# A selective-scan mixer on one core: dt, B and C from h by folded weights, a shorter softplus series, two units moved between engines, a new order

## The reference, cut to what matters

```
h  = layernorm(x) * (1 + ca) + sa                     # 16 x 512 x 256
xz = h @ W_in.T ;  x_ssm, z = split(xz)               # 512 channels each
B, C = x_ssm @ W_B.T, x_ssm @ W_C.T                   # 16 states each
dt = softplus(x_ssm @ W_dt.T + b_dt)                  # 512 channels
# for every time t, channel d, state n:
s[d,n] = exp(dt[d] * A[d,n]) * s[d,n] + dt[d] * B[n] * x_ssm[d]
y[d]   = sum_n s[d,n] * C[n]
y = (y + x_ssm * D) * silu(z)
x = x + ga * (y @ W_out.T) * sigmoid(output_gate)
```

## Time and profile before

| | us |
|---|---|
| median of three runs | 4714.47 (4711.55 to 4716.5) |
| the profiled execution | 4710.14 |
| its span | 4708.4 |
| granted TensorE clock, mean over the span | 0.972 |
| setup, until the first load of x is issued | 35.45 |
| first scan starts | 114.78 |
| last scan starts | 1960.91 |

### The profile page before, as it was taken

One profiled execution on the slowest core, in us unless ns is written; L12 is line 12 of the kernel. 1 busy time (PEld: TensorE's weight loads), 2 busy tenths in 40 slices (PEclk: granted clock), 3 DMA queues, 4 the chain that ended last, 5 costly groups with the idle time before them and its releaser, 6 DMA issues. The chain is left out here.

```text
span 4708.4 us, 60762 instructions
## 1 busy us (share of the span) xinstructions
PE 4365.9 (93%) x19870; PEld 2651.1 (56%) x19870; DVE 3755.0 (80%) x6094; ACT 2731.8 (58%) x5844; POOL 2231.3 (47%) x1060
## 2 busy tenths in 40 slices
PE   5999999999999999649999999999999999999997
PEld 3444444444444444226676767676666667676665
DVE  2999999999999999667777777777777777777773
ACT  3666666666666666215555656564656556565653
POOL 1999999999999999612111111111111111111110
PEclk7999999999999999869999999999999999999999
DMA  1233333333333333330000000001010000001000
GB/s 65 104 113 113 113 112 113 113 117 116 113 116 114 113 112 108 108 112 9 24 14 28 14 28 15 28 14 54 14 67 19 28 28 24 31 19 37 19 32 23
DMA packets 112567, 299.37 MB, mean 64 GB/s; under 512 B 18940, under 2 KB 39008, under 8 KB 111488
## 3 DMA queue, kind: packets, MB, share of 16 engines
q1 hardware_dynamic: 104240, 283.46, 17.7%
q10 hardware_dynamic: 8016, 12.03, 0.7%
HBM read 254.81 MB, written 40.63 MB: 63 GB/s over the span
## 5 line engine op out<-in xcount | busy, mean ns | idle before, releaser
L840 POOL TENSOR_TENSOR a_state<-a_state,a_c_wide 128x1024 f32<-128x1024 f32 x512 | 1195.5, 2364 | 11.7 <-DVE a_state L780 9.9
L561 PE MATMUL a_y_sum<-a_state,a_ident 128*128 128x512 f32 x2048 | 960.6, 610 | 11.3 <-POOL a_state L840 11.2
L1446 POOL TENSOR_TENSOR b_by_cos<-b_qk,b_rotary 128x1024 f32<-128x1024 f32 x128 | 306.7, 2396 | 1164.0 <-DVE b_qk L1488 1164.0
L1210 PE MATMUL b_bank<-b_w_qkv,b_hx_part 128*128 128x512 f32 x2304 | 635.8, 414 | 111.4 <-DVE b_hx_part L1465 62.6
L780 DVE TENSOR_TENSOR_SCAN a_state<-a_decay,a_slot 128x1024 f32<-128x1024 f32 x320 | 722.1, 2277 | 11.9 <-PE a_y_sum L561 5.1
L561 PEld LDWEIGHTS a_y_sum<-a_state,a_ident 128*128 128x128 f32 x2048 | 395.1, 195 | 449.5 <-issue 355.1
L1452 POOL TENSOR_TENSOR b_rate_wide<-b_row_rate,b_one 128x512 f32<-128x512 f32 x128 | 133.0, 1039 | 1061.3 <-DVE b_row_rate L1544 1055.2
L1381 ACT ACTIVATE b_scores<-b_scores,b_row_bias 128x256 f32<-128x256 f32 (+1 forms) x1024 | 477.7, 469 | 154.7 <-DVE b_row_bias L1534 154.7
L1323 PE MATMUL b_bank<-b_hn_part,b_w 128*128 128x512 f32 x2112 | 526.5, 402 | 28.8 <-ACT b_gelu L1427 22.1
L1210 PEld LDWEIGHTS b_bank<-b_w_qkv,b_hx_part 128*128 128x128 f32 x2304 | 416.5, 191 | 232.9 <-DVE b_qk L1488 72.2
L697 ACT ACTIVATE a_slot<-a_dt,a_neg_a 128x512 f32<-128x512 f32 x384 | 249.7, 683 | 404.8 <-DVE a_state L780 404.8
(11 more groups left out here) (202 smaller groups left out, 7173.8 us busy)
## 6 DMA issues: line engine op xcount, KB each, us to landing
a_c_wide<-bc_rows SPq DMA_DIRECT2D x256, 512.0 KB, 3.6
a_b_wide<-bc_rows SPq DMA_DIRECT2D x96, 512.0 KB, 4.7
b_hx<-stack_rows SPq DMA_DIRECT2D x64, 256.0 KB, 4.0
b_x_res<-stack_rows SPq DMA_DIRECT2D x32, 512.0 KB, 4.5
a_xt<-in_L_attn_x SPq DMA_DIRECT2D x16, 512.0 KB, 6.7
x_rows<-a_x_t SPq DMA_DIRECT2D x16, 512.0 KB, 6.2
stack_rows<-a_h_t SPq DMA_DIRECT2D x16, 512.0 KB, 5.9
stack_rows<-b_xc SPq DMA_DIRECT2D x16, 512.0 KB, 2.9
```

What stands on the lines that cost most here:

```text
L561: last = nc.tensor.matmul(y_sum[dd][:], ident[:], state[state_ring.slot[q]][:, i, :], start=False, stop=(j == GROUPS - 1 and i == GROUP - 1))
L840: nc.gpsimd.tensor_tensor(h[:], h[:], c_wide[c_ring.slot[q // 2]][:], ALU.mult).then_inc(cmul_done.sem, 1)
L1210: last = nc.tensor.matmul(psum.tile(name)[:], x[:, c, w * P:(w + 1) * P].bitcast(F32R), weights[:, c, cols:cols + INNER].bitcast(F32R), st ...
L1446: nc.gpsimd.tensor_tensor(by_head(by_cos), by_head(qk), for_heads(rotary[layer][:, w, 0], DIM_HEAD), ALU.mult)\
```

## The change

- **Folded weights.** h @ W_in.T @ W_dt.T is h @ (W_dt W_in).T. The setup now forms the products of W_dt, and of W_B and W_C, with the x_ssm half of W_in on PE (8 + 8 fp32 matmuls), and cuts them into upper and lower float32r parts. In the pass dt, B and C come from `h_upper` and `h_lower` by three float32r products over 256 inputs, as z does, in place of an fp32 product over the 512 channels of x_ssm. Their steps wait for h to be cut, and no longer for the copies of x_ssm; in return the next sequence's h is not cut before dt, B and C are done.
- **Series.** It ends at the cubic term, w((w/sqrt(3) - sqrt(3)/4)^2 + 13/16) = w(1 - w/2 + w^2/3). The square is formed on ACT, in place of the linear term, and DVE is left with one instruction and the copy under the mask.
- **Pool units.** `POOL_LOADS = (1, 4, 6, 9, 12)`: the pool units are 2, 3, 8, 9, 12, 13, 18, 19, 24, 25, that is ten of 32; units 28 and 29 now belong to DVE, PE spreads their B, and one load of B less is made.
- **Order.** The table `MIXER_ORDER` is another one.

```diff
-POOL_GROUPS = (1, 4, 6)
+POOL_LOADS = (1, 4, 6, 9, 12)
+SERIES_ROOT = 3.0 ** 0.5
...
-xs-:0 xscopy-:1 xload:0 hcut-:0 cmul-:5 cmul-:6 mul-:9 decay-:11 xs-:1 bcast-:11 hcut-:1 bcast-:12 sum-:7 cload:0
...
+sum-:5 bcast-:10 sum-:6 mul-:12 mul-:13 xload:0 bcast-:11 scan-:12 cload-:13 cload-:14 cload-:15 scan-:13 cload:0
...
-        by_pool = [q for q in units if unit(q)[0] in POOL_GROUPS]
+        by_pool = [q for q in units if q // 2 in POOL_LOADS]
...
-            def product_of_parts(to, at, signal):
+            def product_of_parts(to, parts, at, rows, signal):
...
-                upper, lower = w_in_t
+                upper, lower = parts
                 pairs = [(weights, x, c) for weights, x in ((upper, h_upper), (lower, h_upper), (upper, h_lower))
                          for c in range(CHUNKS)]
...
             def project_bc(s, slot, _):
-                wait(pe, xs_done, s, INNER_CHUNKS)
+                wait(pe, h_cut, s, CHUNKS)
                 banks.wait_free(pe, s, "bc0")
-                product(bank("bc0")[0:2 * STATES, :], cols(w_bc_t, 0, 2 * STATES), chunks(xs[slot]), bc_full)
+                product_of_parts(bank("bc0")[0:2 * STATES, :], w_bc_in, 0, 2 * STATES, bc_full)
 
             def project_dt(s, slot, half):
-                wait(pe, xs_done, s, INNER_CHUNKS)
+                wait(pe, h_cut, s, CHUNKS)
                 banks.wait_free(pe, s, f"dt{half}")
                 for dd in range(2):
-                    product(work[:, dd, :], cols(w_dt_t, (2 * half + dd) * P), chunks(xs[slot]), dt_full)
+                    product_of_parts(work[:, dd, :], w_dt_in, (2 * half + dd) * P, P, dt_full)
...
             def cut_upper(s, slot, c):
                 wait(act, z_full, s - 1, INNER_CHUNKS)
+                wait(act, dt_full, s - 1, INNER_CHUNKS)
+                wait(act, bc_full, s - 1, 1)
...
-                nc.scalar.activation(sp_p[:], work[:], ACT.Identity, scale=-0.25, bias=third[:])
+                nc.scalar.activation(sp_p[:], work[:], ACT.Square, scale=1.0 / SERIES_ROOT, bias=root[:])
...
-                nc.vector.tensor_tensor(sp_p[:], sp_p[:], work[:], ALU.mult).then_inc(series_done.sem, 1)
-                step(1)
-                nc.vector.scalar_tensor_tensor(sp_p[:], sp_p[:], -0.5, work[:], ALU.add, ALU.mult).then_inc(series_done.sem, 1)
-                step(2)
-                nc.vector.scalar_tensor_tensor(work[:], sp_p[:], 1.0, work[:], ALU.add, ALU.mult).then_inc(series_done.sem, 1)
-                step(3)
+                nc.vector.scalar_tensor_tensor(work[:], sp_p[:], 13.0 / 16, work[:], ALU.add, ALU.mult).then_inc(series_done.sem, 1)
+                wait(dve, series_done, s, half + 1)
...
+                pe.wait_ge(copied, len(turns))
+                for weights, cols, at in ((w_dt_t, D_INNER, 0), (w_bc_t, 2 * STATES, 2)):
+                    for c in range(CHUNKS):
+                        for k in range(INNER_CHUNKS):
+                            last = nc.tensor.matmul(banks[at + c][:, 0:cols], w_in[:, k, c * P:(c + 1) * P], weights[:, k, :],
+                                                    start=(k == 0), stop=(k == INNER_CHUNKS - 1))
+                        last.then_inc(folded, 1)
                 pe.wait_ge(w_mod_loaded, 16)
```

More of the change, by code:

```diff
@@ new lines @@
+cload:12 bcast-:25 z-:2 mul-:29 bcast-:26 z-:3 scan-:28 cmul-:25 cmul-:26 cmul-:27 norm:0 cmul-:28 cmul-:29 bcast-:27
+h2store:0 sum-:22 dt-:1 cmul-:30 bcast-:28 scan-:29 sum-:23 bcast-:29 mul-:30 sum-:24 mul-:31 sum-:25 xcopy:0 decay:6
+bcast-:30 scan-:30 bcast-:31 sq2:0 sum-:26 sum-:27 scan-:31 bload+:1 mul:0 sum-:28 decay:7 mul:1 bcast:0 bcast:1
+sum-:29 step-:1 dev2:0 cmul-:31 decay:8 bcast:2 gate-:2 scan:0 mul:2 gate-:3 scan:1 xcopy:1 scan:2 scan:3 decay:9
+mul:3 mul:4 res:0 sum-:30 mod:0 cmul:0 scan:4 sum-:31 skip:0 decay:10 out:0 bcast:3 res:1 cmul:1 bcast:4 mul:5 out:1
@@ L166 @@
+dtadd-:1 sum:0 bcast:5 up:0 cmul:2 scan:5 xT:0 bcast:6 mod:1 cen2:0 decay:11 up:1 cmul:3 cmul:4 mean2:0 decay:12 mul:6
+sum:1 cmul:5 mul:7 scan:6 bcast:7 mul:8 scan:7 xn2:0 decay:13 bload+:4 scan:8 xscopy:0 sum:2 decay:14 decay:15
+decay:16 xscopy:1 h2:0 scan:9 mul:9 xscopy:2 bcast:8 cmul:6 var2:0 bccopy:0 mul:10 xT:1 hcut:0 mul:11 cmul:7 cmul:8
+sum:3 cmul:9 sum:4 hcut:1 scan:10 scan:11 bcast:9 hT:0 decay:17 bcup:0 hT:1
 """
@@ L1818, in _ @@
                         nc.vector.tensor_tensor(lower.bitcast(F32R), full, upper, ALU.subtract).then_inc(copied, 1)
+                for i, (parts, c, cols) in enumerate((parts, c, cols) for parts, cols in ((w_dt_in, D_INNER), (w_bc_in, 2 * STATES))
+                                                     for c in range(CHUNKS)):
+                    upper, lower = parts
+                    full = banks[i][:, 0:cols]
+                    dve.wait_ge(folded, i + 1)
+                    nc.vector.tensor_copy(upper[:, c, :].bitcast(F32R), full).then_inc(fold_upper, 1)
+                    dve.wait_ge(fold_upper, i + 1)
+                    nc.vector.tensor_tensor(lower[:, c, :].bitcast(F32R), full, upper[:, c, :], ALU.subtract)
                 dve.wait_ge(a_step, 1)
```

58 lines of the change are left out of this document (26 added, 32 removed).

## The result

| | before | after |
|---|---|---|
| median of four runs beside each other | 4713.01 us | 4596.62 us |
| spread of the runs | 4711.54 to 4716.5 | 4593.07 to 4598.76 |
| profiled execution, its span | 4710.1, 4708.4 | 4595.64, 4593.9 |

The change makes the kernel faster: the ratio is 0.9751, with an interval of 0.9737 to 0.9764.

A forecast was written before the change was run, and what follows sets the result against it. DVE, POOL and PE bound the period side by side, PE making the others wait. Fifteen periods -79, last pass -4, setup and fill -5: -88 on 4710.1 gives 4622, forecast 4626 after 4.4 us for the median; range 4602 to 4672.

The forecast's parts named there:

- The series: Polynomial on DVE, twice per pass: two instructions fewer in each half, 2.48 us each time, -4.96 us a period.
- Two units of u*B: Two units moved from POOL to DVE: DVE gains 2.4 us a period, POOL falls from 111.65 to 107.0.
- the adjacency: Order on DVE: units whose scan directly follows their u*B fall from five to two, -0.45 us a period.
- W: DVE's waits left in a period: between 0.5 and 3.5 us, taken as 1.3.
- the gates, the residuals and the mean: DVE's waits for PE there: 1.0 us each at paired gates and residuals, 0.5 at the mean, expected to go.
- units 21, 23 or 27: DVE's u*B there: the spread of B from PE can be late by a few tenths of a microsecond.
- The POOL margin of one microsecond: Before unit 13's scan: POOL needs 35.3 us, DVE arrives after some 36; most likely the next thing late.
- Setup, fill and last pass: Outside the fifteen periods: setup +13 us and fill -18, together -5; last pass -4.
- The margins at dt: PE's dt halves against DVE: first 3.5 us of work within 5.0, no wait; second a margin of 1.0 us.
- Moved waits: Rival: second u*B of eight pairs waits 0.3 us for its spread; period 115.3, 4696 us; chance 0.11.
- POOL as the bound: Rival: POOL's 107.0 us plus 4.3 idle set the period at 111.3; 4635 us; chance 0.10.
- The clock: Rival: idle PE drops to its lower clock, deciding from 16 us low per period; 4791 at 40 us; chance 0.05.

The follow-up runs named there:

- b1: The kernel before with the folded products only, its order, series and twelve POOL units kept: 4719.1 us, ratio 1.001.
- a5: The changed kernel with 12 more PE matmuls ahead of each half of dt, their result overwritten: 4692.6 us, ratio 0.995.
- c3: The changed kernel with a third of the dt products, only upper weights by upper h: 4623.3 us, ratio 0.980.
- c4: The changed kernel without half of the sums over the states, so y lacks half of its terms: 4650.8 us, ratio 0.987.

## Why the prediction was right and wrong

**The bound.** Right in the main: DVE, POOL and PE side by side, with PE making the others wait. But b1 took 7 us of PE's work away and gained nothing, so it was not the amount of that work that made them wait. DVE is what is left (108.5 of 109.0), as forecast, and silu's starts were to be 110 to 111.5 apart and are 109.0.

**The series and the u*B.** The series was priced at -4.96; its instructions took 10.01 us a period and now take 4.96, by the distance of their starts, -5.05. Two units of u*B were +2.4 with -0.45 for the adjacency, +1.95. They measured 23.64 us for twenty and 25.16 for twenty-two, +1.5: the second of a pair costs 1.12 whatever follows it. The scans lost another 0.36. In all DVE's own work fell by 3.6 (112.4 to 108.8) where 3.0 stood in the sum. POOL came out at 107.8 for 107.0.

**The waits: this is the step that failed.** W was taken as 1.3 us and is 0.2, below the lower bound of 0.5. At the gates, the residuals and the mean the waits went, as forecast, though for the gates the cause given was not the whole one (see the clock, below). The rest, "a few tenths" at units 21, 23 or 27, did not come; 0.17 is all. The POOL margin of one microsecond held too: no scan waited for POOL in that period. In the sum the error in W and the one in DVE's work are 1.1 + 0.6 = 1.7 us a period, 25 of the 28 us that were missing. The rows show every spread but one in time; which part of the change did that, no run separates.

**Setup, fill and last pass.** Setup cost +11.5 at the cut of h for +13, the fill gave -20.2 (62.8 to 42.6 us from the cut to the first scan) for -18: -8.7 for -5. The last pass gave -7.3 for -4; it has the period's savings in full. What follows the last scan took 5.4 back, which stood at nothing.

**The margins at dt.** They were right for the first spread behind each half and wrong as margins: the next spread had 0.3 us at the first half (932.84 + 0.59 = 933.4 against DVE's 933.7) and none at the second. It did no harm here. It would have, had the products been any dearer: a5 paid 96 us, where the margins said 33 to 63.

**Moved waits, and POOL as the bound.** Neither happened. The pairs have eight spreads that could be late and one was.

**The clock.** I gave it 0.05 and the price "from 16 us at the low level per period", with PE's total against DVE's. The rival did not come: the changed kernel's pass ran at 1.00. But its price was wrong. In c3 falls of a few microseconds (0.59 in the stretch of 4 us above) go with a period that is 1.8 us longer: a fall counts as soon as the next spread is late for DVE, long before PE is full. The kernel before was paying this already. In the earlier trace rows its spread behind the 2.91 us still took 0.59, which I took for the whole answer. What follows it are these rows of PE, of DVE and of a stretch of 4 us:

```profile
1035.22 10.44 PE L561 MATMUL a_y_sum<-a_state,a_ident 128*128 128x512 f32 x20
```

```profile
1045.70 0.69 DVE L786 TENSOR_TENSOR a_u<-a_y_sum,a_sz 128x512 f32<-128x512 f32 x1 [1.02 <-PE a_y_sum L561]
```

```profile
1036.00:1040.00 4.00, 4.00 (x7) 1.59 (x6) 3.93 (x4) 3.94 (x18) 4.00 (x2) 0.60 0.28 92
```

The twenty sums took 10.44 us, where b1's at full clock took 8.75: 1.69 us too long, and the second gate waits 1.02 us for them. So the wait of 1.0 us at the gates, for which the prediction blamed only that they stand in a pair, would not have been there at full clock, as far as these rows tell. It is so all through the mixer of the kernel before: in its rows of PE from 240 to 1900 us these twenty sums took from 9.76 to 11.41 us, and the other twenty of a period, which follow no such stretch, 8.75 each time. The sum had no line for that, in either direction. In the changed kernel no stretch of PE in the period is above 1.59 us and the level holds; but c3 fell after 1.58 us, so the length of the stretch alone is not the reason. How much of the 1.1 us in W comes from the clock was not measured by itself.

The Trainium skill, "TensorE: Matmul & The Clock Gate", section "HAM oscillation — how this bites in real kernels", says that matmuls in bursts with gaps keep falling back to the low rate. I wrote that the pass disagreed with it. The pass of the kernel before agrees with it, by the 0.60 in the stretch above, and so do c3 and c4: 0.59 in a 4 us stretch of c3, 0.88 over ten periods of c4. The kernel after, at 1.00, has gaps too and does not fall back.
